# Graph propagation on one core: products in chunks of 1024 columns instead of 512

## The reference, cut to what matters

```python
# third layer, three times             # fourth layer, ten times
msgs = norm[:, None] * x[row]          agg = segment_sum(h[s] * wn[:, None], d, n)
x = segment_sum(msgs, col, n)          h = (1.0 - ALPHA) * agg + ALPHA * feat_0
```

## Time and profile before

| | |
|---|---|
| median of 3 runs | 3262.86 us (3261.7 to 3263.56) |
| profiled execution, its time | 3265.59 us |
| its span, first to last instruction | 3263.5 us |
| TensorE busy in the span | 2372.9 us (73%) |
| VectorE, ScalarE, GpSimd busy | 1366.4, 409.0, 1537.4 us |
| loads of d_w | 312 of 1024 KB, from 2273.4 to 3226.6 us |
| issue to landing of such a load | min 5.0, median 8.9, max 15.1 us |
| granted TensorE clock, mean over the span | 0.849 of full speed |

### The profile page before, as it was taken

One profiled execution on the slowest core, in us unless ns is written; L12 is line 12 of the kernel. 1 busy time (PEld: TensorE's weight loads), 2 busy tenths in 40 slices (PEclk: granted clock), 3 DMA queues, 4 the chain that ended last, 5 costly groups with the idle time before them and its releaser, 6 DMA issues.

```text
span 3263.5 us, 51520 instructions
## 1 busy us (share of the span) xinstructions
PE 2372.9 (73%) x16771; PEld 1650.8 (51%) x16771; DVE 1366.4 (42%) x2537; ACT 409.0 (13%) x940; POOL 1537.4 (47%) x1633
## 2 busy tenths in 40 slices
PE   2476667777666546666666666664996999999997
PEld 1466666666666536555555555552432433333332
DVE  1555555555555245545555555545843111111112
ACT  1111111111111111111111111111000000000000
POOL 1577777777777657777777777760000000000000
PEclk8687788778888668888888888885998999999998
DMA  2422221222222212222222222221996999999996
GB/s 41 50 44 43 43 43 43 43 43 43 43 43 44 42 41 55 53 53 54 53 54 53 54 53 53 54 48 45 370 349 241 341 346 353 349 354 352 348 351 227
DMA packets 387169, 433.52 MB, mean 133 GB/s; under 512 B 184958, under 2 KB 197887, under 8 KB 384046
## 3 DMA queue, kind: packets, MB, share of 16 engines
q1 hardware_dynamic: 324860, 352.87, 33.3%
q0 software_dynamic: 51712, 53.06, 8.5%
q10 hardware_dynamic: 10546, 26.89, 2.2%
HBM read 401.00 MB, written 28.43 MB: 132 GB/s over the span
## 4 chain that ended last, share of the span: by engine, by line
PE 36%; POOL 32%; issue 16%; DMA 8%; DVE 4%; SPq 1%; ACT 1%; POOLq 1%; DVEq 0%; ACTq 0%
POOL arena L567 32%; PE bank L1357 26%; DMA arena<-d_p,arena 4%; PE bank L1215 3%; PE bank L1332 2%; DMA arena<-in_edge_weight 2%; PE bank L1183 1%; DMA arena<-d_t,arena 1%; PE bank L1361 1%; PE bank L1227 1%; DVE arena L655 1%; PE bank L1198 1%; DVE arena L697 1%; ACT arena L1031 1%; POOLq L366 0%
## 5 line engine op out<-in xcount | busy, mean ns | idle before, releaser
L1357 PE MATMUL bank<-arena 128*64 128x512 f32 (+1 forms) x4368 | 890.9, 543 | 59.2 <-DVE arena L882 33.3
L567 POOL DMA_INDIRECT arena<-d_t,arena x808 | 764.2, 946 | 299.7 <-issue 250.8
L567 POOL DMA_INDIRECT arena<-d_p,arena x808 | 764.4, 946 | 281.3 <-issue 255.2
L1227 PE MATMUL bank<-arena 128*128 128x200 f32 x3136 | 673.8, 375 | 0.0
L1227 PEld LDWEIGHTS bank<-arena 128*128 128x128 f32 x3136 | 653.5, 226 | 18.4 <-DVE arena L686 3.9
L1357 PEld LDWEIGHTS bank<-arena 128*64 128x64 f32 x4368 | 318.5, 136 | 543.6 <-issue 464.2
L1215 PE MATMUL bank<-arena 128*64 128x47 f32 x3232 | 300.1, 273 | 375.8 <-ACT arena L1031 375.6
L1215 PEld LDWEIGHTS bank<-arena 128*64 128x64 f32 x3232 | 274.4, 176 | 424.4 <-ACT arena L1031 215.8
L697 DVE TENSOR_TENSOR arena<-bank,arena 128x512 f32<-128x512 f32 x202 | 139.8, 692 | 764.3 <-DMA arena<-d_t,arena 414.5
L686 DVE TENSOR_TENSOR arena<-arena,bank 128x1600 f32<-128x1600 f32 x196 | 356.8, 1820 | 6.8
L1183 PE MATMUL bank<-arena 128*96 128x128 f32 x404 | 83.3, 342 | 343.4 <-DVE arena L658 343.4
(11 more groups left out here) (155 smaller groups left out, 1433.2 us busy)
## 6 DMA issues: line engine op xcount, KB each, us to landing
arena<-d_w SPq DMA_DIRECT2D x312, 1024.0 KB, 8.9
d_w<-arena ACTq DMA_DIRECT2D x24, 1024.0 KB
arena<-d_p,arena POOLq DMA_INDIRECT x808
arena<-in_edge_attr SPq DMA_DIRECT2D x101, 128.0 KB
arena<-d_t,arena POOLq DMA_INDIRECT x808
arena<-arena SPq DMA_DIRECT2D x392, 8.0 KB
arena<-in_src SPq DMA_DIRECT2D x202, 4.0 KB
arena<-d_q SPq DMA_DIRECT2D x202, 11.8 KB
```

Of the source, the lines that this page charges most:

```text
L567: g.indirect_dma_start(G[:, b, j, :], None, table, bass.IndirectOffsetOnAxis(ap=idx[:, b, j:j + 1], axis=0)).then_inc(r.g[b], 16)
L1227: last = t.matmul(prod[:, :, WIN * w:WIN * w + WIN], alo[:, b, TPW * w + j, :], outer[:, b, TPW * w + j, :].rearrange("p (c j) -> p c j", ...
L1357: last = t.matmul(banks[t_ % 4][F * (n % 2):F * (n % 2) + F, 0:w_], old[:, n, :], right, start=n < 2, stop=False)
```

## The change

A big chunk is now 1024 columns: `NBIG` = 3 of them per product, and `CORDER` = [0, 3, 1, 2] with number 3 the small chunk. Both column groups take the same row block n: group g multiplies it with the g-th half of the 1024 columns, so partitions 0 to 63 of the bank hold the first 512 columns and 64 to 127 the second, complete. The small chunk still alternates its blocks. One bank, one copy and one turn of four transposes now serve 1024 columns; VectorE gets eight blocks of nodes at once and has no halves to add (except in the small chunk). The pieces in the ring stay as they are, six slots of 1 MB, but are loaded in the order in which they are used now: piece 2q + g is blocks 9 + 4q to 12 + 4q of half g, and a pair of pieces is used together. The turn stands after the fourth block everywhere (`TURN_AT` = 3). The wait for x's last chunk stands at block 16 (`LATE`). Two waits of TensorE on `xs_v` and `acc_c` are gone.

```diff
-TURN_AT = 5
+TURN_AT = 3
-CORDER = [0, NCH] + list(range(1, NCH))
-NPOS = NCH + 1
+NBIG = NCH // 2
+CORDER = [0, NBIG] + list(range(1, NBIG))
+NPOS = NBIG + 1
+LATE = 2 * 4 * (NBIG - 1)
+STEPS = [0, 2, 5, 7]
+NSTEP = 9
...
-        post = at(take(4 * F), 4, F)
+        post = at(take(8 * F), 8, F)
...
             def load_piece(j):
-                c, part = j // NPC, j % NPC
+                c, part = 2 * (j // (2 * NPC)) + j % 2, j % (2 * NPC) // 2
...
             def piece_used(k, j):
-                c, part = j // NPC, j % NPC
+                c, part, g = j // (2 * NPC), j % (2 * NPC) // 2, j % 2
                 if part == NPC - 1:
                     sp.wait_ge(s.acc_t, NPOS * k + CORDER.index(c) + 1)
                 else:
-                    sp.wait_ge(s.pc_free, (NPC - 1) * (NCH * k + c) + part + 1)
+                    sp.wait_ge(s.pc_free, 2 * (NPC - 1) * (NBIG * k + c) + 2 * part + g + 1)
...
-                sp.wait_ge(s.deg_v, j + 1 + (j >= NPC))
+                sp.wait_ge(s.deg_v, j + 1 + (j >= 2 * NPC))
...
-                    n = 4 if c < NCH else 1
-                    lo_ = 4 * c
+                    n = 8 if c < NBIG else 1
+                    lo_ = 8 * c
+                    done = NSTEP * k + STEPS[t_]
...
-                        d.tensor_tensor(y, prod[:, :, 0:F], old[:, lo_:lo_ + n, :], ALU.add).then_inc(s.post_v, 1)
-                    v.wait_ge(s.post_v, 3 * (NPOS * k + t_) + 1)
-                    d.tensor_tensor(y, prod[:, :, F:P], y, ALU.add).then_inc(s.post_v, 1)
-                    v.wait_ge(s.post_v, 3 * (NPOS * k + t_) + 2)
-                    steps(k, t_, lo_, n, y, old, new)
...
+                    if c < NBIG:
+                        if steps is step2:
+                            d.tensor_copy(halves(y), prod).then_inc(s.post_v, 1)
+                        else:
+                            d.tensor_tensor(halves(y), prod, halves(old[:, lo_:lo_ + n, :]), ALU.add).then_inc(s.post_v, 1)
+                        v.wait_ge(s.post_v, done + 1)
+                        steps(k, done + 2, lo_, n, y, old, new)
...
-                if t_ >= 4 or t_ < 0:
-                    pe.wait_ge(s.xs_v, NPOS * k + t_ - 3)
...
-                    if t_ >= 4:
-                        pe.wait_ge(s.acc_c, NPOS * k + t_ - 3)
                     for n in range(NB):
-                        piece = NPC * c + (n - RES) // PIECE
-                        if n == 20 and t_ == 0 and not first:
+                        if n == LATE and t_ == 0 and not first:
                             pe.wait_ge(s.xs_v, NPOS * k)
...
+                        for g in range(2 if c < NBIG else 1):
+                            piece = 2 * (NPC * c + (n - RES) // PIECE) + g
+                            if c == NBIG:
+                                right = Wres[:, n, NCH * CH:NCOL] if n < RES else W6[:, n - RES, :]
+                            elif n < RES:
+                                right = Wres[:, n, CH * (2 * c + g):CH * (2 * c + g) + CH]
+                            else:
+                                if (n - RES) % PIECE == 0:
+                                    pe.wait_ge(s.pc[piece % RING], 16 * (NPIECE // RING * k + piece // RING + 1))
+                                right = ring[:, piece % RING, :].rearrange("p (q a e) -> p a q e", q=CH // QC, e=QC)[:, (n - RES) % PIECE, :, :]
+                            if c < NBIG:
+                                last = t.matmul(banks[t_ % 4][F * g:F * g + F, :], old[:, n, :], right, start=n == 0, stop=n == NB - 1)
+                                if n < NB - 1 and n >= RES and (n - RES) % PIECE == PIECE - 1:
+                                    last.then_inc(s.pc_free, 1)
...
-                        if n == (RES - 1 if t_ else TURN_AT) and not (t_ == 0 and first):
+                        if n == TURN_AT and not (t_ == 0 and first):
                             turn_chunk(k, t_ - 1)
```

More of the change, by code:

```diff
@@ L897, in sums @@
                     return
-                if k == 0 and c == NCH:
-                    d.tensor_reduce(deg_str[:, c, :], W6, AX, ALU.add).then_inc(s.deg_v, 1)
+                if k == 0 and c == NBIG:
+                    d.tensor_reduce(deg_str[:, NCH, :], W6, AX, ALU.add).then_inc(s.deg_v, 1)
                 elif k == 0:
-                    for j in range(NPC * c, NPC * c + NPC):
+                    for j in range(2 * NPC * c, 2 * NPC * c + 2 * NPC):
                         v.wait_ge(s.pc[j % RING], 16 * (j // RING + 1))
-                        part = (j % NPC) * PIECE
-                        d.tensor_reduce(deg_str[:, c, part:part + PIECE],
+                        part = j % (2 * NPC) // 2 * PIECE
+                        d.tensor_reduce(deg_str[:, 2 * c + j % 2, part:part + PIECE],
                                         ring[:, j % RING, :].rearrange("p (q a e) -> p a q e", q=CH // QC, e=QC),
@@ L928, in post_chunks @@
-                    v.wait_ge(s.post_v, 3 * (NPOS * k + t_) + 1)
-                    d.tensor_tensor(y, prod[:, :, F:P], y, ALU.add).then_inc(s.post_v, 1)
-                    v.wait_ge(s.post_v, 3 * (NPOS * k + t_) + 2)
-                    steps(k, t_, lo_, n, y, old, new)
-            def step2(k, t_, lo_, n, y, old, new):
+                    if c < NBIG:
[5 more added lines that the diff above has]
+                        steps(k, done + 2, lo_, n, y, old, new)
+                    else:
+                        if steps is step2:
+                            d.tensor_copy(y, prod[:, 0, :, :]).then_inc(s.post_v, 1)
+                        else:
+                            d.tensor_tensor(y, prod[:, 0, :, :], old[:, lo_:lo_ + n, :], ALU.add).then_inc(s.post_v, 1)
+                        v.wait_ge(s.post_v, done + 1)
+                        d.tensor_tensor(y, prod[:, 1, :, :], y, ALU.add).then_inc(s.post_v, 1)
+                        v.wait_ge(s.post_v, done + 2)
+                        steps(k, done + 3, lo_, n, y, old, new)
@@ L934, in step2 @@
+            def step2(k, done, lo_, n, y, old, new):
                 d.tensor_tensor(y, y, by_node(dinv, lo_, n), ALU.mult).then_inc(s.post_v, 1)
-                v.wait_ge(s.post_v, 3 * (NPOS * k + t_) + 3)
+                v.wait_ge(s.post_v, done)
                 d.tensor_tensor(new[:, lo_:lo_ + n, :], y, by_node(dinv, lo_, n), ALU.mult).then_inc(s.xs_v, 1)
@@ L940, in step3, with step @@
             def step3(a):
-                def step(k, t_, lo_, n, y, old, new):
+                def step(k, done, lo_, n, y, old, new):
                     d.tensor_tensor(y, y, by_node(a, lo_, n), ALU.mult).then_inc(s.post_v, 1)
-                    v.wait_ge(s.post_v, 3 * (NPOS * k + t_) + 3)
+                    v.wait_ge(s.post_v, done)
                     d.tensor_tensor(new[:, lo_:lo_ + n, :], y, gb[:, lo_:lo_ + n, :], ALU.add).then_inc(s.xs_v, 1)
@@ L1325, in turn_chunk @@
                 pe.wait_ge(s.acc_c, NPOS * k + t_ + 1)
-                if t_ >= 4 or t_ < 0:
-                    pe.wait_ge(s.xs_v, NPOS * k + t_ - 3)
                 slot = t_ % NPOS
                 c = CORDER[slot]
-                for n in range(4 if c < NCH else 1):
-                    left = accS[:, slot % 3, P * n:P * n + P] if c < NCH else accL
+                for n in range(4 if c < NBIG else 1):
+                    left = accS[:, slot % 3, P * n:P * n + P] if c < NBIG else accL
                     last = t.transpose(banks[4 + slot % 4][:, P * n:P * n + P], left, ident)
@@ L1340, in product @@
                 for t_, c in enumerate(CORDER):
-                    w_ = CH if c < NCH else LASTW
-                    if t_ >= 4:
-                        pe.wait_ge(s.acc_c, NPOS * k + t_ - 3)
                     for n in range(NB):
-                        piece = NPC * c + (n - RES) // PIECE
-                        if n == 20 and t_ == 0 and not first:
+                        if n == LATE and t_ == 0 and not first:
                             pe.wait_ge(s.xs_v, NPOS * k)
[L1348 to L1364, removed]
-                        if n == (RES - 1 if t_ else TURN_AT) and not (t_ == 0 and first):
@@ new lines, in product @@
+                        for g in range(2 if c < NBIG else 1):
[4 more added lines that the diff above has]
+                                right = Wres[:, n, CH * (2 * c + g):CH * (2 * c + g) + CH]
+                            else:
+                                if (n - RES) % PIECE == 0:
+                                    pe.wait_ge(s.pc[piece % RING], 16 * (NPIECE // RING * k + piece // RING + 1))
+                                right = ring[:, piece % RING, :].rearrange("p (q a e) -> p a q e", q=CH // QC, e=QC)[:, (n - RES) % PIECE, :, :]
+                            if c < NBIG:
+                                last = t.matmul(banks[t_ % 4][F * g:F * g + F, :], old[:, n, :], right, start=n == 0, stop=n == NB - 1)
+                                if n < NB - 1 and n >= RES and (n - RES) % PIECE == PIECE - 1:
```

(8 more changed lines are left out.)

8 lines of the change are left out of this document (4 added, 4 removed).

## The result

The changed kernel takes 3285.89 us (median of 4 runs, 3284.43 to 3287.26) against 3262.82 us before: a ratio of 1.0071, 95% interval 1.0053 to 1.0088. It is slower by 23.1 us; 3287 was forecast. The profiled execution took 3287.26 us, 21.7 more than the one of before. Not all of that comes from the stage of the products.

A forecast was written before the change was run, and what follows sets the result against it. TensorE was taken to bound the products' stage. To the profiled 3265.59 us came -28.3 (turns), +4.3 (small chunk), +1.0 (VectorE) and +46.8 (late piece), +23.8 in sum; with the median 2.7 us lower, 3287 us, range 3238 to 3330.

The forecast's parts named there:

- Matmuls: Block products of a big chunk: 25 pairs, 21.55 us, as two old chunks together, so nothing gained or lost.
- Turns: Transposes at chunk ends: three turns of 0.725 us fewer in each of 13 products, 28.3 us less.
- The small chunk: Chunk of 64 columns: five blocks move behind its turn, 0.33 us more per product, 4.3 us in all.
- 12.5 pairs: Matmuls of an old full chunk: 24 whole blocks and one halved, overlapping in two column groups, 10.775 us.
- the sum of 2.96 us: Small chunk before the change: what six chunks of 11.50 us leave of a 71.96 us product.
- VectorE: Operations bare only behind each layer's last product: about 0.6 and 0.4 us more, together 1.0 us.
- The sums beside product 0: VectorE's 24 sums, eight per big chunk, 18.2 us plus posts, worked off in time for nearly all refills: no cost.
- The late piece: Second piece of each big chunk's fourth pair arrives late, TensorE waits 1.2 us in 39 chunks: 46.8 us more.
- 0.9 beside 1.4: Two lateness estimates for that second piece, from stage-start and running-stage landings, in us; 1.2 was taken between them.
- the 7.1 us from the first issue: Time the fourth pair was said to have from its first issue; landing within it would mean no stall.
- No stall, 3240 us: Rival for the fourth pair: it lands in time, so the turns pay, faster by 0.7%; chance 0.18.
- The fourth, DMA alone as the pace: Rival for big chunks: the queue restarts badly or loses time, stalls beyond 2.3 us, 3345 us and more; chance 0.10.

The follow-up runs named there:

- the first three experiments: Changed kernel with one resident block between first and second pair, 3263.24 us; resident blocks spread between pairs, 3231.04; 512 KB pieces in twelve slots, 3271.49.
- the spread kernel: The changed kernel with its nine resident blocks spread between the pairs of pieces (3, pair, 2, pair, 2, pair, 2, pair): 3231.04 us, ratio 0.9900.
- one block between: The changed kernel with resident block 8 taken between the first and second pair of every big chunk: 3263.24 against 3264.31 us for the kernel before.
- with two: The changed kernel with resident blocks 7 and 8 between the first and second pair: 3757.55 against 3778.67 us for the kernel before in its set.
- the half pieces: The changed kernel with pieces of two blocks (512 KB) in a ring of twelve slots: 3271.49 us, ratio 1.0022 to the kernel before.

## Why the prediction was right, point by point

**The sign and the size** were right, 3287 against 3285.9 us, and so was the mechanism. But that the two agree to 1 us is luck, twice over: two terms of the sum were off by more than 10 us each, in opposite directions, and the stage of the products took 26.4 us more in the trace, not 23.8, while the edge phases happened to be 4.7 us shorter. (In the profiled executions of the first three experiments, which have the same edge phases, the first load came at 2271.3, 2271.9 and 2272.5.) By terms (13 products, 39 big chunks):

**Matmuls** at no cost: right. Two groups on the same block overlap; the weight loads keep their 0.43 us beat.

**Turns**, -28.3 us: right. The full chunk without stall is 22.26 us (22.275 forecast), and doubling the transposes cost what it should.

**The small chunk**, +4.3 us: it became 2.76 instead of 2.51 us, 3.2 us in all, by the cause that was given.

**A gain that was missed.** The forecast let 12.5 pairs fill every chunk of 512 columns before. That holds where one chunk's odd block finds its partner in the next, but behind the small chunk one block per product ran alone, for 11.94 - 11.20 = 0.74 us: some 10 us in all, which the change removes because both groups take the same block. The turn moved to the eighth block showed it in the kernel before. The row was there: the copies of the earlier trace rows have 11.94 us for this chunk. I used them only in the sum of 2.96 us for the small chunk, which hid the 0.44 us that they stand above 11.50. Without stall the change is therefore worth some 35 us by its steady products and not 23: 13 x (71.96 - 69.24) = 35.4, 33.3 measured.

**VectorE** at the two ends, +1.0 us: no run tried it by itself, but the traces give about half. From the last copy of a full chunk to the end it is 21.54 us before and 21.89 in the changed kernel; the stretch over the layer norm is 28.63 us longer than a product before and 28.77 in the spread kernel. The sums beside product 0, put at nothing, show no cost in the changed kernel. In the spread kernel the first two products end 145.5 us after the first load, against 148.4 before: 2.9 us gained, where two steady ones gain 5.4. TensorE waits for d_w there, 5.7 us in 9 waits and in no later product, and VectorE does too; what of this is the sums and what the start of the ring was not tried.

**The late piece**, +46.8 us: the place, the piece and the recurrence were right, its price was not. The step that failed is that the second piece "has 6.90 + 0.43 - 0.64 = 6.69 us" from its own issue. The first piece has that; the second is needed by the other group at the same time (at 2784.77 the row has both groups' weight loads, x2), while SyncE issues it 0.49 us later. So it has 6.2 us. With a median of 7.56 us to land it is late by some 1.3, four of the 39 landings are 0.9 to 1.6 us later still, and the mean stall is 1.52, not 1.2: 39 x 1.52 = 59 us. I had put 0.9 beside 1.4 and taken a value between; with 6.2 us in place of 6.7 the row of 0.9 would have said 1.4.

Together: 13 x (73.79 - 71.96) = +23.8 us by products, as forecast, of which -35.4 without stall and +59.2 of stall. The forecast had -23.0 (its other terms) and +46.8. What is left of the 26.4 us lies in the start of the stage, the stretch over the layer norm and the end; it was not taken apart.

**The rivals.** The same slip stands in the 7.1 us from the first issue, inside which the pair was to be there: both groups need their pieces after 6.7. No stall, 3240 us, did not come, but is what the spread order makes of the same change. One argument for it was misread: the row has the first data in the third half-microsecond slice, 1.0 to 1.5 us after the issue and not about 2. The pairs seen here are both there after 0.49 + 7.4 = 7.9 us at best as two loads, 8.1 at best as one. The page of the Trainium skill ("DMA: Bandwidth & Descriptors", section "Anatomy of one DMA — SWDGE (gpsimd) path") gives 2.0 us and the bytes at 436 GB/s, so about 6.8 us for 2.1 MB, an estimate. The traces disagree with its size for these loads of SyncE's, and against the 6.7 us that there really are it would have meant a stall of 0.1 us and not none. The fourth, DMA alone as the pace, is refuted for whole pieces by the spread kernel (364 GB/s with no wait), and is what happens to half ones.

How the stall shrinks with more blocks between is less than one for one (0.70 for the first 0.86, 0.48 for the next). The landings say how: the second load of the fourth pair takes longer from its own issue, 7.70 us on the mean in the changed kernel, 7.92 with one block between and 8.09 with two, and single ones take 9 to 10. What makes them slip was not tried.

## What to carry to other kernels

When a change makes two buffers of a ring be used together, ask for each refill which work stands between the moment its slot comes free and the moment it is needed, and hold that against the time from issue to landing on an almost empty queue, with the second issue's delay included. A mean rate that fits says nothing about that; work that needs no transfer, put between, repaired it here at no cost. A total that fits says little about its terms: take the stage's own length from the trace before calling a sum right. Where two halves of an engine run side by side, count per half from one common stop to the next: an odd number there is a hole that the sum of blocks does not show.

## What was not expected of the hardware

The DMA engines had room although the profile's page had them at 99% and more: the kernel before moved 351 GB/s at a share of 1.00, the spread kernel 364 at 1.01, the half pieces 348 with the share at 1.09. And one load of 2 MB onto a near empty queue took 8.1 to 9.7 us, median 8.6, where two loads of 1 MB were both there after a median of 8.05.
